# The second projection of the next tile moved directly behind the first one on TensorE

## The reference, cut to what matters

```python
def attn_layer(x, Wqkv, qs, ksc, Wo):
    qkv = x @ Wqkv                       # 128 -> 3 * 1024
    q, k, v = jnp.split(qkv, 3, -1)      # 16 heads of 64
    q = l2norm(q) * qs
    k = l2norm(k) * ksc
    q = q * cos * scale + rotate_half(q) * sin * scale
    k = k * cos * inv + rotate_half(k) * sin * inv
    out = local_attention(q, k, v)       # windows of 32 keys back, softmax
    return out @ Wo

for i in range(DEPTH):                   # 6
    x = attn_layer(shift_tokens(x), ...) + x
    x = ffn_layer(shift_tokens(x), ...) + x
```

## Time and profile before

| | |
|---|---|
| median of 3 runs | 2151.84 us |
| the profiled execution | 2149.59 us |
| its span, first to last instruction | 2147.8 us |
| mean granted TensorE clock | 0.973 |
| PE busy (matmuls) | 1932.7 us, 90% |
| PEld busy (weight loads) | 1460.9 us, 68% |
| DVE busy | 1676.1 us, 78% |
| POOL busy | 1662.5 us, 77% |
| ACT busy | 1604.5 us, 75% |

### The profile page before, as it was taken

How to read it: one execution, slowest core, us unless ns; L and a number is a source line. 1 busy time by engine, 2 the same in 40 slices (tenths; PEclk the granted TensorE clock), 3 DMA queues, 4 the chain that set the end, 5 groups by cost and what they waited for, 6 DMA issues and landing times.

```text
span 2147.8 us, 67396 instructions
## 1 busy us (share of the span) xinstructions
PE 1932.7 (90%) x22192; PEld 1460.9 (68%) x22192; DVE 1676.1 (78%) x4006; ACT 1604.5 (75%) x5607; POOL 1662.5 (77%) x1251
## 2 busy tenths in 40 slices
PE   5992999998999988999988999988999988999986
PEld 3761777774777774777774777774777774777772
DVE  4666888886888876888876888876888876988865
ACT  4872888884888874888884888874888885888872
POOL 2124999985999976899976899976899976999960
PEclk9995999999999999999999999999999999999998
DMA  2001321110311111211111211111211111112210
GB/s 63 13 12 50 82 55 44 44 45 25 88 44 44 44 45 38 76 44 44 44 45 41 74 44 44 44 45 42 73 44 44 44 45 35 46 44 49 54 28 20
DMA packets 44547, 99.43 MB, mean 46 GB/s; under 512 B 7344, under 2 KB 24208, under 8 KB 43504
## 3 DMA queue, kind: packets, MB, share of 16 engines
q1 hardware_dynamic: 44400, 97.59, 17.8%
HBM read 19.59 MB, written 1.05 MB: 10 GB/s over the span
## 4 chain that ended last, share of the span: by engine, by line
PE 27%; DVE 26%; issue 18%; ACT 18%; POOL 8%; DVEq 1%; POOLq 0%; ACTq 0%; DMA 0%; SPq 0%
ACT prob L485 10%; DVE n2c L791 6%; DVE n L784 5%; DVE ts_ L794 5%; ACT nat L501 4%; PE bank L1115 3%; PE bank L1149 3%; DVE tc_ L787 3%; DVE nmax L741 3%; PE bank L1122 3%; ACT kT L523 2%; PE bank L1151 2%; PE bank L1150 2%; POOL rn L319 2%; POOL ropeL L356 2%
## 5 line engine op out<-in xcount | busy, mean ns | idle before, releaser
L319 POOL TENSOR_TENSOR rn<-n2c,half_neg 128x8 f32<-128x8 f32 x384 | 632.8, 1648 | 129.5 <-DVE n2c L791 128.7
L485 ACT ACTIVATE prob<-bank,nmax 128x96 f32<-128x96 f32 x1536 | 504.1, 352 | 131.0 <-DVE nmax L741 130.8
L321 POOL TENSOR_TENSOR tsum<-tc_,ts_ 128x512 f32<-128x512 f32 x384 | 489.9, 1276 | 0.0
L324 POOL TENSOR_TENSOR w_nat<-tsum,rn 128x512 f32<-128x512 f32 x384 | 400.6, 1043 | 37.8 <-POOL tsum L321 15.1
L784 DVE TENSOR_REDUCE n<-nat 128x8 f32<-128x512 f32 x384 | 262.5, 683 | 140.9 <-ACT nat L501 138.2
L485 ACT ACTIVATION_READ_ACCUMULATOR prob<-bank,nmax 128x1 f32 x1536 | 334.3, 218 | 0.0
L1149 PE MATMUL bank<-w_hi,xs 128*128 128x512 f32 x576 | 277.0, 481 | 34.2 <-DVE ts_ L794 13.1
L494 ACT ACTIVATE pT<-bank 96x512 f32<-96x512 f32 x384 | 231.3, 602 | 74.4 <-PE bank L1122 72.3
L501 ACT ACTIVATE nat<-bank 128x512 f32<-128x512 f32 x384 | 233.0, 607 | 72.0 <-PE bank L1151 69.4
L794 DVE TENSOR_TENSOR ts_<-bank,ropeL 128x256 f32<-128x256 f32 x768 | 285.8, 412 | 0.0
L1122 PE MATMUL bank<-idf,prob 128*96 128x128 f32 x1536 | 244.9, 282 | 43.6 <-ACT kT L523 29.5
(11 more groups left out here) (125 smaller groups left out, 3413.7 us busy)
## 6 DMA issues: line engine op xcount, KB each, us to landing
vspace<-v_nat SPq DMA_DIRECT2D x96, 384.0 KB, 4.0
vspace<-v_nat SPq DMA_DIRECT2D x96, 256.0 KB, 3.4
vspace<-v_nat SPq DMA_DIRECT2D x95, 128.0 KB, 2.3
nat<-w_qkv SPq DMA_DIRECT2D x5, 1536.0 KB, 8.5
wo<-w_o SPq DMA_DIRECT2D x6, 512.0 KB, 4.0
w<-w SPq DMA_DIRECT2D x6, 341.0 KB, 3.0
shared<-w_qkv SPq DMA_DIRECT2D x1, 1536.0 KB, 6.8
w<-w SPq DMA_DIRECT2D x6, 192.0 KB, 3.0
```

The lines of the kernel that those rows point to most:

```text
L319: nc.gpsimd.tensor_tensor(rn[:, r, :], n2c[:, r, :], half_neg[:, 0:8], ALU.pow).then_inc(pool_step, 1)
L321: nc.gpsimd.tensor_tensor(tsum[:, r, :], tc_[:, r, :], ts_[:, r, :], ALU.add).then_inc(pool_step, 1)
L324: nc.gpsimd.tensor_tensor(w_nat[:, r, :].rearrange("p (h d) -> p h d", d=D), tsum[:, r, :].rearrange("p (h d) -> p h d", d=D), rn[:, r, :] ...
L485: last = nc.scalar.activation(prob[:, 4 * b + i, :], SB[b][:, i * SPAN:(i + 1) * SPAN], ACT.Exp, bias=nmax[:, p, 8 * G + 4 * b + i:8 * G + ...
```

## The change

In PE's `tile`, `project(t + 1, 1 - p, 1)` moves up, directly behind `project(t + 1, 1 - p, 0)`, ahead of heads 2 and, where the tile isn't an opening one, ahead of transpose_out of t-1 and project_out of t-1. In the closing tile nothing changes, since it projects nothing. The orders of ACT, DVE, POOL and SP stay as they are.

```diff
                     else:
                         project(t + 1, 1 - p, 0)
+                        project(t + 1, 1 - p, 1)
                     if opening:
                         eng.wait_ge(tp_free, t * 4 + 1)
                     else:
...
                         project_out(t - 1, 0)
                     if closing:
                         transpose_in(1)
-                    else:
-                        project(t + 1, 1 - p, 1)
                     eng.wait_ge(tp_free, t * 4 + (2 if opening else 3))
                     transpose_heads(t, 3, 4)
```

## The result

The changed kernel took 2153.63 us (median of 20 runs, 2150.61 to 2158.08), the kernel before 2150.62 us in the same comparison (20 runs); the ratio is 1.0018, with a 95% interval of 1.0009 to 1.0026. That is 2 to 6 us more: within the 0.5% that the prediction counted as no change, though the interval lies wholly above 1. The prediction was 2155, and 1.2 us of its distance comes from where it started: it took 2151.84 for the kernel before, the median of three runs, where twenty give 2150.62.

What follows compares the result with a forecast made beforehand. It took POOL as nearly full (93%) and a ring through n2c(2), which ends with tsum, as setting the period. 84 x 0.04 = 3 us on the profiled 2149.59 gave 2152.6, with 2.25 for the median 2155; range 2143 to 2203.

Steps and rivals of the forecast that it cites:

- the slack of n2c(2): On DVE ahead of ts_(2): n2c(2) takes 1.27 us, ending with POOL's tsum(1), where it needs 0.17 elsewhere.
- the sum: Total over the 84 middle tiles: 0.04 us each makes 3 us; the opening tiles were taken as 0.
- rival B: n2c(1) starts after POOL's w_nat and is held to its end: 0.81 a tile, 68 us, 2220; chance 0.15.
- Step 1: PE: heads 2, the o_nat transposes and the output product come 0.72 us later; nothing behind them is lost.
- Step 2: ACT: heads 2 and all following work, square 1 included, come 0.58 to 0.63 us later, 0.60 taken.
- the sign: ACT: about 0.6 us of idle time ahead of heads 2, where there was none.
- Step 3: DVE: n2c(1) starts 0.60 later but takes 0.17 instead of 0.51 us, so ts_(1) is only 0.26 late.
- Step 4: PE: projection 3 is 0.40 us late, projection 4 0.04 a tile, by ACT's bounds 0.00 to 0.07.
- Step 5: Rest of the tile: n2c(2) still starts inside tsum(1), ts_(2) doesn't move; ACT's idle 0.47 ahead of square 3 is used up.
- Rival C: The chain through ACT decides: the 0.60 lands in full, 50 us, 2202, or in parts, 2165 to 2200; chance 0.19.
- ring of n2c(2): Waits said to set the period: tsum(1), n2c(2), ts_(2), projections 4 and 5, heads, scores, square 0, n2c(0), rn, tsum.
- Rival D: Opening tiles: the longer matmul batch keeps the clock at 1.00 instead of 0.74, 11 us faster, 2144; chance 0.06.

Runs made afterwards that it cites:

- behind_h2: The change with projection 1 one place later, behind heads 2 and ahead of the o_nat transposes: 2152.96 us, ratio 1.0023 to the kernel before.
- behind_out: The change with projection 1 two places later, directly ahead of the output product, at its old place in opening tiles: 2152.15 us, ratio 1.0011 to before.
- after_dose: The changed kernel with the first matmul of projection 1 issued twice, 0.23 us more PE work: 2219.07 us, ratio 1.0322 to the kernel before.
- after_no_clamp: The changed order with the 1e-24 floor (n2c) left out, so POOL's power reads n2 itself: 2148.81 us, ratio 0.9995 to the kernel before.
- before_no_clamp: The kernel before with the 1e-24 floor (n2c) left out, so POOL's power reads n2 itself: 2098.14 us, ratio 0.9771 to the kernel before.
- The pair with the reduction: The floor made by a tensor_reduce over pairs instead of the tensor_scalar: 2109.09 us in the order of before, 2151.13 us in the changed order.
- before_clamp_reduce: The kernel before, its floor kept but made by a tensor_reduce over pairs instead of the tensor_scalar: 2109.09 us, ratio 0.9813 to before.

## Why the prediction was right

The mechanism came out as written, the slack of n2c(2) taking up the delay of ACT. Two things about the number are luck. The middle tiles cost 6.4 us, where the sum says 3, and the whole time hides this, since the rest came out shorter. And in nearly half of the middle tiles n2c(1) started within 0.03 us of where rival B begins, which was priced at 0.81 a tile.

Step 1: 0.72 of shift on PE. Heads 2 now load 1.27 behind projection 0 (979.96 and 978.69), before it was 0.57 (1011.16 and 1010.59): 0.70. Heads 3 had their transposes long ahead of ACT, and nothing behind them was late.

Step 2: ACT 0.58 to 0.63 late. It is 0.57 in odd tiles and 0.65 in even ones, both outside the bounds by 0.01 to 0.02, and rival B was said to begin at 0.66. The idle time ahead of heads 2 is 0.46, where about 0.6 was named as the sign: heads 2 used to follow square 0 by 0.49 where that lasts 0.60, and the idle time counts from its end. The even tiles are the term that I had a little too low: their first instruction behind a wait comes 0.08 us later than in odd tiles (0.67 against 0.59 from the maxima to the first exponential, before and after alike), and I had read the wait's latency in an odd tile alone.

Step 3: n2c(1) at 0.17, and the hold lost as slack. It takes 0.16, and ts_(1) is late by 0.22 (0.26 said). In even tiles it starts 0.01 behind w_nat, where I had put it 0.04 ahead; that it still gets through is luck that I hadn't reckoned with. The nearest starts that were held lie 0.024 and 0.025 behind a w_nat (one tile each in the traces of behind_h2 and behind_out), the latest free ones 0.021.

Step 4: projection 3 late by 0.40, and 0.00 to 0.07 a tile at projection 4, 0.04 taken. Projection 3 is late by 0.37 in the odd tile shown (8.20 from the maxima for 7.83). Even tiles pay 0.09, by which their delay passes the slack of 0.56, and odd ones next to nothing, together 3.3 us over tiles 2 to 13, which is the 3 us of the sum. Missed were 3.2 us in tiles 1 and 14: I had counted them as like the others, and had read one tile's timeline only. In five of them n2c started 0.08 to 0.11 elsewhere against POOL than in the others, before the change already.

Step 5: n2c(2) still inside tsum(1). It is, 0.60 behind tsum's start, and takes 0.70. The idle time ahead of square 3 is used up to nothing, as said.

Rival B didn't come true in the whole and did in two tiles, at 0.83 where it was priced at 0.81. after_dose brings it in all of them: 2219 for the 2220 that was written. Rival C is refuted in this kernel, by the same ring of n2c(2), and is what happens once that ring is cut: the delay of 0.50 costs 0.46. Rival D, the clock: the openings sum to 106.20 after and 104.81 before, with 103.6 to 107.8 in the others, so no gain is seen. The traces say what varies them: in all thirteen of them an opening tile takes 15.2 to 17.0 us where the granted clock over it is 1.00, and 18.1 to 19.9 where it is 0.73 to 0.91. That of the fourth layer has 0.74 before and after; that of the third went from 0.82 to 0.74. So the longer batch shows no gain in the clock in this trace.

The shape of the answer rests on after_no_clamp and before_no_clamp together: the same move costs 6 us in the middle tiles with the hold in place and 51 without it. The pair with the reduction says the same with 46, and no DVE instruction is left out there. That the move seemed nearly free was the hold's doing.

## What to carry to other kernels

Before work is put forward on an engine, ask which engine waits for what it is put ahead of, and follow that delay to the ring that sets the period, taking off the slack at each step; here 0.7 on PE became 0.6 on ACT, 0.4 at projection 3 and less than 0.1 at projection 4. A move that is free beside a stall shows its price when the stall is removed, so the stall has to go first: here it was worth 45 us of middle tiles with the order left alone and 5 in the moved order. And read every kind of tile, the peeled ones too: an edge that the odd tiles clear by 0.07 us the tiles 14 of two layers miss by 0.12.

## What the runs showed of the hardware

Whether a small DVE tensor_scalar is held by a POOL instruction is decided within some 0.02 us: started 0.01 behind w_nat it ran free in 0.16 (and w_nat took 1.07 for 1.04), started 0.03 behind tsum it was held for 1.27, started 0.12 behind w_nat for 0.96. Over all the traces with this instruction, 71 starts up to 0.021 behind w_nat ran free and every one from 0.024 to 0.55 was held to its end; behind tsum starts from 0.011 to 0.016 ran free and others from 0.014 on were held. A tensor_reduce with one input at the same place in the code was never held (384 times, 0.164 at most). The Trainium skill, SBUF — State Buffer, section Who interferes with whom, says that a tensor_reduce never contends with GpSimd on this chip; these rows agree.

Not every POOL instruction holds. In the trace of before, copy_prev, a tensor_scalar of 128x256, runs inside rn, the power; it does so 89 times, started 0.35 to 1.33 behind rn, and never takes over 0.35:

```profile
1022.22 0.34 DVE L766 TENSOR_SCALAR kT<-kT,follows 128x256 f32<-128x256 f32 x1
...
1021.87 1.65 POOL L319 TENSOR_TENSOR rn<-n2c,half_neg 128x8 f32<-128x8 f32 x1
```

and in before_clamp_reduce, where it falls inside w_nat, it takes 0.95 and ends 0.15 behind w_nat's end:

```profile
972.44 0.95 DVE L766 TENSOR_SCALAR kT<-kT,follows 128x256 f32<-128x256 f32 x1
...
972.20 1.04 POOL L324 TENSOR_TENSOR w_nat<-tsum,rn 128x512 f32<-128x512 f32 x1
```

The same section speaks of the pair as taken for the whole of an instruction; the 1.65 us of rn aren't taken in that way. It reads 8 elements a partition, w_nat 512, and it is a power where w_nat is a product. Which of the two counts, or whether rn touches its operands in a small part of its 1.65 us only, no run here shows; the time that POOL's record spans isn't what decides.
